# Row gathers on GpSimd: the small write behind each gather goes, a wait for a landing comes in at pair starts

## The reference, cut to what matters

```
xt  = einsum('nd,rde->rne', x, W)                            # first and second sum, 8 relations
agg = segment_sum(xt[rel, src], dst, num_segments=12500)
out = relu(agg + x @ SW + b)

agg = segment_sum((relu(x @ W1 + b1) * dinv)[src], dst, ...)  # third sum, no relations
```

## Time and profile before

| | us |
|---|---|
| median of 3 runs | 7358.1 (7354.17 to 7372.18) |
| profiled execution, span from the first to the last instruction | 7320.2 |
| first sum, POOL's first to its last gather | 4.5 to 2422.3 |
| second sum, the same | 2466.8 to 4874.1 |
| third sum, the same | 4902.1 to 7297.5 |
| POOL busy | 5851.5 (80%) |
| PE busy | 3691.2 (50%) |
| DVE busy | 1720.1 (23%) |

### The profile page before, as it was taken

How to read it: one execution, slowest core, us unless ns; L and a number is a source line. 1 busy time by engine, 2 the same in 40 slices (tenths; PEclk the granted TensorE clock), 3 DMA queues, 4 the chain that set the end, 5 groups by cost and what they waited for, 6 DMA issues and landing times.

```text
span 7320.2 us, 56431 instructions
## 1 busy us (share of the span) xinstructions
PE 3691.2 (50%) x13687; PEld 2669.6 (36%) x13841; DVE 1720.1 (23%) x2844; ACT 409.6 (6%) x915; POOL 5851.5 (80%) x9940
## 2 busy tenths in 40 slices
PE   4555555555555556556565555554424333433343
PEld 3333333333333333334343333433323333333333
DVE  4333333333333212222222222221101111111111
ACT  1000000000000100000000000010000000000000
POOL 7888888888888588888888888867888888888887
PEclk7666667676666777767677776675555555555555
DMA  2111111111111112211222221211111111111111
GB/s 66 49 51 52 50 50 50 51 52 50 50 52 51 40 49 57 56 56 55 56 58 56 56 57 56 56 54 42 51 51 52 51 51 51 51 51 53 51 51 48
DMA packets 197585, 382.88 MB, mean 52 GB/s; under 512 B 84322, under 2 KB 93326, under 8 KB 197542
## 3 DMA queue, kind: packets, MB, share of 16 engines
q0 software_dynamic: 159456, 326.88, 17.0%
q1 hardware_dynamic: 36416, 54.67, 2.1%
q10 hardware_dynamic: 1670, 0.85, 0.0%
HBM read 356.43 MB, written 25.65 MB: 52 GB/s over the span
## 4 chain that ended last, share of the span: by engine, by line
POOL 48%; issue 20%; another core or an unknown queue 20%; PE 7%; DVE 3%; DVEq 1%; POOLq 0%; ACT 0%; DMA 0%; ACTq 0%; SPq 0%
POOL rows L794 39%; POOL pause L798 9%; PE bank L980 3%; PE bank L950 3%; DVE r_S L1042 1%; DVE r_hot L1037 1%; PE bank L1205 1%; ACT r_agg L904 0%; PE bank L1440 0%; PE bank L964 0%; DVE acc L1081 0%; DMA acc<-in_dst_dram 0%; DVEq L1071 0%; POOLq L109 0%
## 5 line engine op out<-in xcount | busy, mean ns | idle before, releaser
L794 POOL DMA_INDIRECT rows<-in_x_dram,idx x1661 | 1588.6, 956 | 466.9 <-issue 396.7
L794 POOL DMA_INDIRECT rows<-x_d,idx x1647 | 1574.2, 956 | 453.5 <-issue 397.8
L794 POOL DMA_INDIRECT rows<-h_d,idx x1640 | 1566.9, 955 | 441.4 <-issue 396.3
L980 PE MATMUL bank<-r_S,rows 128*128 128x128 f32 x6644 | 1408.2, 380 | 705.1 <-issue 486.8
L1205 PE MATMUL bank<-r_S,rows 128*128 128x64 f32 x3322 | 821.9, 388 | 1332.3 <-issue 1079.4
L980 PEld LDWEIGHTS bank<-r_S,rows 128*128 128x128 f32 x6644 | 1299.5, 285 | 501.4 <-issue 482.1
L1205 PEld LDWEIGHTS bank<-r_S,rows 128*128 128x128 f32 x3322 | 775.1, 315 | 1378.0 <-issue 1272.4
L798 POOL MEMSET pause<- 128x128 f32 x4948 | 1096.3, 222 | 4.3 <-issue 0.2
L1042 DVE TENSOR_TENSOR r_S<-bank,key 128x1792 f32<-128x1792 f32 x238 | 480.4, 2019 | 1225.9 <-remote 1080.3
L964 PEld LDWEIGHTS bank<-zeros_bf 128*128 128x128 bf16 x476 | 54.1, 114 | 1463.0 <-issue 1056.8
L964 PE MATMUL bank<-zeros_bf 128*128 128x512 bf16 x323 | 174.9, 542 | 722.4 <-issue 505.8
(11 more groups left out here) (152 smaller groups left out, 1471.1 us busy)
## 6 DMA issues: line engine op xcount, KB each, us to landing
rows<-in_x_dram,idx POOLq DMA_INDIRECT x1661, 3.3
rows<-x_d,idx POOLq DMA_INDIRECT x1647, 3.4
rows<-h_d,idx POOLq DMA_INDIRECT x1640, 3.4
d_xr<-in_x_dram SPq DMA_DIRECT2D x54, 218.0 KB
x_d<-d_yr SPq DMA_DIRECT2D x27, 218.0 KB
d_x1r<-x_d SPq DMA_DIRECT2D x27, 218.0 KB
h_d<-d_hr SPq DMA_DIRECT2D x27, 218.0 KB
part_d<-d_pr SPq DMA_DIRECT2D x27, 218.0 KB
```

Source lines behind the costliest of these rows:

```text
L794: pool.indirect_dma_start(out=self.c.rows[:, self.place(s), :], out_offset=None, in_=self.table[:, :], in_offset=bass.IndirectOffsetOnAxis ...
L980: mm = pe.matmul(agg_ps[j][:, bass.ds(offs[j * KG + k], TK)], c.rows[:, g.place(h * KG + k), :], S[:, pb, j * KG + k, :], start=False, sto ...
```

## The change

The buffer c.pause, the memsets, the semaphore `paused` and the waits for it go. In their place POOL calls `breathe` at some pair starts, after the waits for the indices and for `summed`: it waits until the group issued last, the last group of the pair before, has landed. In a sum's first pass that is at pairs 1, 2 and 3; after that at pairs 0 and 2 of a pass in the first two sums, and at pair 0 alone in the third.

```diff
-        c.pause = sb("pause", [P, PT, P])
...
-        self.rest = PAIR if then is None else 1
+        self.rests = (0,) if then is None else (0, PR // 2)
...
-        self.paused = sem("paused")
...
+    def breathe(self, pool, i, p):
+        pool.wait_ge(self.landed[p * PAIR - 1 if p else RING - 1], (i + 1 if p else i) * (KG * 16))
+        gate(pool, self.c.passed)
...
-        rest = self.rest
...
-        def iteration(q, i, part, set_of, skip=0):
+        def iteration(q, i, part, set_of, skip=0, first=False):
             at = set_of * UN
             for p in part.pairs:
                 if (p + 1) * PT <= skip:
-                    pool.sem_inc(self.paused, PAIR // rest)
                     continue
                 pool.wait_ge(self.idx_ready, (q * (IT + 1) + i) * PR + p + 1)
                 pool.wait_ge(self.summed, self.pairs_summed(q, i, p))
                 gate(pool, self.c.passed)
+                if p > 0 if first else p in self.rests:
+                    self.breathe(pool, i, p)
                 for h in range(p * PAIR, (p + 1) * PAIR):
-                    if (h + 1) * KG <= skip:
-                        if h % rest == rest - 1:
-                            pool.sem_inc(self.paused, 1)
-                        continue
-                    if h % rest == 0:
-                        pool.wait_ge(self.paused, q * (NG // rest) + i * (RING // rest) + h // rest + 1)
-                        gate(pool, self.c.passed)
                     for k in range(part.of(h)):
                         s, slot = h * KG + k, h if k < halves(part, h) else RING + h % PAIR
                         if s < skip:
                             continue
                         pool.indirect_dma_start(
...
                         ).then_inc(self.landed[slot], 16)
-                        ins = pool.memset(self.c.pause[:, s % PT, :], 0.0)
-                    if h % rest == rest - 1:
-                        ins.then_inc(self.paused, 1)
...
-            iteration(q, 0, FULL, 0, skip)
+            iteration(q, 0, FULL, 0, skip, True)
...
-        pool.sem_inc(self.paused, 1)
...
-        pool.wait_ge(self.paused, rounds * (NG // rest) + 1)
-        gate(pool, self.c.passed)
```

## The result

The kernel after takes **7442.0 us** (median of 4, 7430 to 7449) where the kernel before takes 7356.1 us (7340 to 7372): a ratio of **1.0114, 95% interval 1.0095 to 1.0132**, 1.1% slower. Forecast were 6949 us, with 6834 to 7140 as the range, 0.91 for faster and 0.07 for slower.

The account below looks back on a forecast made before the run. POOL was taken as the bound, by its gathers, memsets and stops between them. From the profiled span, 7320 - 425 - 378 - 45 + 439 = 6911 us, plus 37.9 for the median gives 6949 us; range 6834 to 7140.

Parts of the forecast that it names:

- The memsets: POOL's pause writes between gathers: dropping them saves 0.086 us at each of 4948 gathers, 425 us less.
- The waits for `paused`: POOL's waits after groups for the last memset: 590 waits of 0.64 us go, 378 us less.
- The landing waits: POOL's new waits at pair starts for the last group to land: 154 at 2.85 us, 439 us more.
- my lower end: Low price of a landing wait, from PE's release 2.55 us after a gather's start: 2.1 us each, 323 in all.
- estimate of 2.15 us to a landing: Skill page's rule for a 65 KB gather; by it a wait costs 1.7 us and the time is 6772 us.
- PE's stalls: POOL's 70 us of waits for PE at a full ring should mostly go: 45 us less, net.
- First sum: some 15 us: POOL's idle time in the first sum, less its own waits, leaves some 15 us of waiting for PE.
- Second sum: leaves nothing: POOL's idle time in the second sum, less its own waits, leaves no waiting for PE.
- What brings this pace back is what the change adds: Argument against PE as bound: PE's quick pace returned at a 3.88 us POOL stop, and the change adds such stops.
- 2.3 us for a pair: PE's claimed time for a third-sum pair at its quick pace, against 32.5 us in slow stretches.
- PE becomes the bound in the first and third sum: Rival: these sums keep their passes, only the second gains 118 us: 7240 us, halfway 7095; chance 0.17.
- The unbroken stream starves PE: Rival: without small stops PE slows, above all in the third sum; 7673 us at 100 us a pass; chance 0.07.

Follow-up runs that it names:

- e1: Kernel before with one pause write per group (per pair in the third sum) instead of per gather, waits kept: 6764.2 us, ratio 0.9475 beside 7138.
- e5: Kernel after, unchanged, run again where the kernel before takes 7138 us: 6667.7 us, ratio 0.934.
- e2: Kernel after without any wait for a landing: 6280.8 us, ratio 0.8798, where the kernel before takes 7138 us.
- e6: Kernel before, unchanged, run for its trace in the same place as the unchanged kernel after: 7137.7 us.
- e14: Kernel after with a landing wait ahead of every pair, where the kernel before takes 7349.1 us: 7509.5 us, ratio 1.0212.
- e3: Kernel after with a landing wait ahead of every pair in all sums, where the kernel before takes 7138 us: 7360.8 us, ratio 1.0307.
- e10: Kernel before, memsets and their waits kept, plus the landing waits of the kernel after: 7385.3 us, ratio 1.0219 beside 7225.1.
- e9: Kernel before with the wait for the memset once per pair in all sums, every memset kept: 7337.2 us, ratio 1.0147 beside 7225.1.
- e15: Kernel before with one pause write per group instead of per gather, where the kernel before takes 7349.1 us: 7459.2 us, ratio 1.0134.

## Why the prediction was wrong

**The memsets** (425 us less): right. Gathers start 1.251 us apart in the result's trace, and e1 gave the 375 us worked out for it.

**The waits for `paused`** (378 us less): right. Every second group start of the kernel after comes 1.251 us after the last gather.

**The landing waits** (439 us more): the mechanism right, the size too high. POOL's 111.5 us for 47 waits in e5 are 2.37 us of idle time each, 0.30 of it normal, so 2.07 us: my lower end, taken from the earlier trace rows, not the 2.85 us from the earlier trace rows. In the second sum they are longer (148.8 us for 47, so 2.87 us), which makes 61 x 2.07 + 61 x 2.87 + 32 x 2.07 = 367 us in all, 2.38 each. Taking them all out gave 387 us (e2 against e5), and the late gather of every pass goes with them there (e2's pass is 56 x 1.251 and nothing more).

The earlier trace rows were misread. They are not all gathers of the line: with most updates missing only three of the 4948 have a landing time, the last one of each sum. In e5 and e6 the last gather of the third sum takes 3.31 and 3.32 us too, where the median of that sum is 2.53 and 2.54. Nor is a landing slower in a place with slow steps. In the third sum e14 stands for 3.24 to 3.45 us from start to start at the second pair start of each pass after the first, and e3, in a place without slow steps, for 3.25 to 3.45. One of e14 (timeline of POOL):

```profile
5878.78 0.94 POOL L790 DMA_INDIRECT rows<-h_d,idx  x1 [0.30 <-issue]
5882.13 0.94 POOL L790 DMA_INDIRECT rows<-h_d,idx  x1 [2.41 <-DMA rows<-h_d,idx]
```

and one of e3:

```profile
5749.43 0.94 POOL L790 DMA_INDIRECT rows<-h_d,idx  x1 [0.30 <-issue]
5752.74 0.95 POOL L790 DMA_INDIRECT rows<-h_d,idx  x1 [2.37 <-DMA rows<-h_d,idx]
```

The estimate of 2.15 us to a landing from the Trainium skill's fit ("DMA: Bandwidth & Descriptors", the anatomy of a SWDGE DMA) is too low for the 2.5 us of e5's first and third sum and for the 3.5 of its second. The 1.7 us per wait worked out from it is nearer to the 2.07 of the first and third sum than my 2.85, and farther from the 2.38 over all 154.

These three terms nearly account for e5: 425 + 378 - 367 = 436 us less, where 470 were measured and 409 forecast; the other 34 us stay unexplained. The forecast's fourth term, 45 us of PE's stalls, has nothing to stand for where there are no slow steps.

**"PE's stalls" (45 us less), from "First sum: some 15 us" and "Second sum: leaves nothing"**: this is the step that failed. The starts of the gathers tell what this term became. In the trace of before POOL stands at its pair starts for 18, 2 and 74 us beyond what its own waits explain; in the result's trace, with 2.07 us off for each landing wait, it is 221, 249 and 241 us (e5: 3, 45 and nothing). The term was forecast to fall by 45 us. It rose by 617, or by some 570 without e5's 45, which are the second sum's longer landings. With the 436 us that the other three gain this makes 134 us more, and the span grew by 117.

I read PE's share from POOL's idle time: where POOL hardly ever waited for PE, I took PE to have room. But the ring holds four pairs, about 80 us, and it hid how PE stood. In the first trace ACT's copies, which end PE's work on a group, come 35 to 79 us behind the group's last gather in the first sum (median 55) and 8 to 64 in the second (median 30); in e6 it is 4 to 36 us with medians of about 9. In the first sum PE is never less than 14 us behind a group's last gather once the first pass is over, so it never waits for rows: its own pace was the 81 us of the pass, and when POOL's sank to 76.8, the ring had to fill. In the second sum PE did wait for rows, 164.5 us of 2200, so its own pace was about 75 us a pass, enough for the forecast. There the pace itself fell: in the result's trace PE is 27 us or more behind at every group, waits for no rows, and takes 83 us a pass, with slow steps of 628 us for 191. So two things were wrong: that PE had room, and that its pace would stay. POOL's waits in the result's second sum (2700 to 4700 us) show PE's side too; "remote" is the semaphore `summed` as well:

```profile
POOL rows L790 <- issue: 415.5, 1280, 2.4
POOL rows L790 <- PE bank L970: 130.0, 23, 11.9
POOL rows L790 <- remote: 126.1, 28, 6.1
POOL rows L790 <- DMA rows<-x_d,idx: 54.5, 13, 5.2
```

By these labels POOL waits for PE for nearly five times as long as for landings there (256 us against 54.5), most updates being without a record. For comparison with the earlier trace rows: in e5's third sum PE waits for rows for 1292 of 2148 us.

**"What brings this pace back is what the change adds"**: half right. Stops do bring it back (the timeline above, and e10, e14). But 28 or 56 gathers lie between two of the change's stops, and slow steps mostly began some 5 to 20 gathers after one. And without writes PE got one instruction per gather and not nearly two, which no trace of before could show. The "2.3 us for a pair" at the quick pace was misread as well: it is the time between two additions on DVE. The pair's 28 matmuls took 6.21 us (timeline of PE in the trace of before):

```profile
5781.63 6.21 PE L1205 MATMUL bank<-r_S,rows 128*128 128x64 f32 x28 [1.33 <-issue]
```

**The rivals.** "PE becomes the bound in the first and third sum" (0.17) had the right kind of end, but let the second sum gain and PE keep its pace; it priced 7240 us. "The unbroken stream starves PE" (0.07) had the right cause and side, and the place wrong: the third sum, for which it was made, lost 4 us, the second 61. Its reason for the low chance, that small stops did not end the slow stretches in the kernel before, did not speak against it: e9, which only thins them out, is slower than before. But they are not enough alone: e15, which keeps them and leaves out most writes, is slower too.

## What to carry to other kernels

A producer that seldom waits is no proof that the consumer has room: look how far behind it runs, against the depth of the buffer. Where it never catches up, both set the pace, and a faster producer gives nothing until the consumer is faster. And a pace that was read beside one pattern of the producer need not hold beside another, as the second sum shows.

Before a releaser, a chain or a landing time is read, count how many of the semaphore updates are in the trace. Here the program fixes their number, most were missing in nine of 17 traces, and a figure that was read for all gathers stood for three.

An engine that is idle for "issue" between instructions with no wait between them, in steps of one length, is short of instructions. In these runs that went with the place where the program ran, so a change that packs one queue denser should be timed in more than one place: this one is worth 6.6% where the kernel before takes 7138 us (measured in one of three such places), and costs 1.1% where it takes 7349. The kernel without any landing wait (e2, 6281 us) beats both there by 12% and 5.8%, and is the worst of the four in the 7225 us place; none of the versions that ran in both kinds of place beats the kernel before in both.

## What the runs showed of the hardware

**Places differ.** The kernel before took 7138, 7138 and 7138 us on three chips, 7225 on a fourth and 7349 on a fifth, with ranges of 0.1 to 0.5%; those of the result, 7356 us, look like the fifth. POOL's and DVE's own instructions last the same: a gather 0.953 us in e6 and 0.956 in the first trace. So does the moving of rows: the last of a gather's 32 packets ends 2.20 us after the gather's start, by the median of the first sum, in the result's trace and in e5. What differs is the coming of instructions, and not for PE alone. Of SyncE's 699 register instructions none takes over 0.6 us in e5 and e6 (29.5 us in all); in the first traces 110 and 152 do (108 and 144 us in all), in e10 53, though PE shows no slow steps there. And only in these places are updates of semaphores missing from the trace.

**The time to a landing** is 2.5 us by the median in e5's first and third sum, 3.5 in its second, and 3.3 for the last gather of the third sum in e5, e6 and the first trace. Why the second sum's are longer was not tested.

**What the gathers have to do with the slow steps** is shown by its effect alone: one PE instruction per gather at 1.25 us, nearly two with a write between, a step of 0.70 us from about 4 us after the last gather on, and none 4 us later. No run tells whether the fetching of instructions is held up, or the writing of their records. Against the first speaks that the pages of the result and of e5 count the same 38 packets on the two queues of kind "instruction", with 2396 slow steps in one trace and 102 in the other. For the second speak three things. Every run here was recorded, the timed ones too (each gave spans and clocks). In exactly the places with slow steps 51 to 82% of the gathers' updates have no record. And instructions, updates and packets together make 36 to 40 records per us there, whatever the kernel, against 46 to 53 elsewhere; but that follows in great part from the missing ones. Nor do missing records bring PE's slow steps by themselves: in e10 51% are missing.

The Trainium skill, "NOTIFIC — the notification-queue block", section 7.1, says that inside the block that writes records the hardware always holds its producers back rather than lose one. No trace here shows that block, and records did get lost here, at a stage that no trace names.

If the writing of records is the cause, the loss of 1.1% would be the profiler's, and an execution without records might gain in every place; such a time was not to be had, so this stays open. So does what sets the 0.70 us, and why the (7225) place lies between.
